# Feed-forward loop one tile longer, clears by range, router weights later, attention's dense products spread over steps

## What is computed

```python
x = x + tanh(g_xattn[0]) * softmax_attention(layernorm(x), ctx)   # 32 heads, 8 groups of keys, head size 16, masks
x = x + tanh(g_ffn[0])   * bit_ffn(layernorm(x))                  # 512 -> 2048 -> 512, ternary weights, gelu
x = x + tanh(g_xattn[1]) * linear_attention(layernorm(x), ctx)    # 16 heads, gated
x = x + tanh(g_ffn[1])   * moe(layernorm(x))                      # shared 2048-wide FFN, and 2 of 8 experts
```

## Time and profile before

| what | value |
|---|---|
| median of 3 runs | 1860.0 us (1858.31 to 1861.89) |
| the profiled execution | 1863.76 us, of it 1862.0 us span |
| granted TensorE clock over the span | 0.954 |
| PE busy | 1620.1 us, 87% |
| DVE, ACT, POOL busy | 964.0, 711.3, 823.7 us |
| phase A, phase B | to 534 us; 541 to 865 us |
| phase C, phase D | to 1120 us; 1124 to 1857.5 us |

### The profile page before, as it was taken

The page is one execution under the profiler, slowest core; times in us unless marked ns, Lnnn a source line. Parts: engine busy times, 40 slices in busy tenths (PEclk is TensorE's granted clock), DMA queues, the critical chain, the costliest instruction groups (busy, mean ns, idle before and its releaser), DMA issues. The chain is left out here.

```text
span 1862.0 us, 29494 instructions
## 1 busy us (share of the span) xinstructions
PE 1620.1 (87%) x10826; PEld 831.9 (45%) x10826; DVE 964.0 (52%) x1947; ACT 711.3 (38%) x1311; POOL 823.7 (44%) x853
## 2 busy tenths in 40 slices
PE   4689998999838888976999987999999999888887
PEld 3255555555413343433665643444444444333343
DVE  5566666667445777761556552376554333111136
ACT  2177778778834444441223221121111111222221
POOL 2377787767733444432344334353343431111134
PEclk9899999999759998998999998999999999999999
DMA  5633444332404444343355425464444652466645
GB/s 180 140 102 92 109 90 104 84 67 65 108 15 91 97 102 99 74 77 62 72 120 102 100 52 139 86 156 108 99 111 97 154 107 61 112 150 157 153 142 170
DMA packets 453941, 195.69 MB, mean 105 GB/s; under 512 B 395484, under 2 KB 418270, under 8 KB 453800
## 3 DMA queue, kind: packets, MB, share of 16 engines
q1 hardware_dynamic: 448120, 175.19, 42.0%
q0 software_dynamic: 5680, 18.62, 3.7%
HBM read 77.17 MB, written 22.81 MB: 54 GB/s over the span
## 5 line engine op out<-in xcount | busy, mean ns | idle before, releaser
L1007 POOL TENSOR_TENSOR a_pl<-a_prob,a_ph 128x512 f16<-128x512 f32 x256 | 295.9, 1169 | 103.8 <-ACT a_prob L916 102.9
L1090 DVE TENSOR_REDUCE a_mx<-bank 128x2 f32<-128x512 f32 x256 | 172.7, 686 | 107.7 <-PE bank L643 105.3
L137 PE MATMUL bank<-XTh,d_whs 128*128 128x512 f16 x512 | 194.8, 380 | 2.1 <-issue 1.3
L138 PE MATMUL bank<-XTl,d_whs 128*128 128x512 f16 x512 | 194.5, 380 | 0.0
L139 PE MATMUL bank<-XTh,d_wls 128*128 128x512 f16 x512 | 194.5, 380 | 0.0
L915 ACT ACTIVATE a_ph<-bank 128x512 f16<-128x512 f32 x256 | 153.7, 601 | 87.5 <-PE bank L663 62.8
L2211 POOL CAST d_cut<-d_raw 128x512 f16<-128x512 f32 x90 | 56.8, 631 | 235.5 <-DMA d_raw<-in_L_ffn_sw 153.9
L916 ACT ACTIVATE a_prob<-bank 128x512 f32<-128x512 f32 x256 | 153.9, 601 | 0.0
L2131 DVE TENSOR_TENSOR d_hid<-d_hid,bank 128x512 f32<-128x512 f32 x64 | 44.0, 687 | 182.9 <-PE bank L139 176.1
L1354 PE MATMUL bank<-b_wpj,b_hTh 128*128 128x512 f16 x256 | 105.5, 412 | 25.6 <-DMA b_hTl<-b_hcut 25.6
L1344 PE MATMUL bank<-b_wfc,b_xTh 128*128 128x512 f16 x256 | 98.3, 384 | 32.6 <-DMA b_xTl<-f_cut 25.5
(11 more groups left out here) (330 smaller groups left out, 3978.7 us busy)
## 6 DMA issues: line engine op xcount, KB each, us to landing
d_raw<-in_L_ffn_w SPq DMA_DIRECT2D x48, 256.0 KB, 3.0
d_raw<-in_L_ffn_sw SPq DMA_DIRECT2D x42, 256.0 KB, 3.1
made<-e_y SPq DMA_DIRECT2D x39, 256.0 KB
a_stage<-in_L_ffn_w_fc SPq DMA_DIRECT2D x32, 256.0 KB, 2.9
a_stage<-in_L_ffn_w_proj SPq DMA_DIRECT2D x32, 256.0 KB, 3.1
a_fbuf<-in_ctx SPq DMA_DIRECT2D x16, 256.0 KB, 3.9
rows<-f_cut SPq DMA_DIRECT2D x16, 256.0 KB, 2.5
out_x<-X SPq DMA_DIRECT2D x16, 256.0 KB
```

The source lines that it names most:

```text
L137: nc.tensor.matmul(out_ap, lhi, rhi, start=first, stop=False)
L138: nc.tensor.matmul(out_ap, lhi, rlo, start=False, stop=False)
L1007: nc.gpsimd.tensor_tensor(pl[:, n % NP, :], prob[:, n % 2, :], ph[:, n % NP, :], ALU.subtract).then_inc(ev["L"], 1)
L1090: nc.vector.tensor_reduce(mx[:, h, tt, half, 2 * (g % 4):2 * (g % 4) + 2], bank[BS + m % 2][:, :].rearrange("p (r k) -> p r k", r=2), AX_X ...
```

## The change

1. `phase` clears each run of neighbouring semaphore numbers with one instruction.
2. Phase A: PQ = (15, 21), PK = (19, 25), OUT = (7, 11), OTURN = (5, 6), TURN0 and NEG0 = 27. Products are cut by k: q and output one k (three matmuls) a step over four steps, kv two k (six short matmuls) a step over two steps. The two halves of the output are turned in two steps. SP's `place_q(b+2, 0)` moves to n = 26.
3. Phase B: `hidden_clip` of a tile moves to the start of the next iteration, `result` into the next iteration, and each engine's order changes; on POOL `low(n+1, 3)` moves behind `dev(m)`.
4. Phase D: the router's transposes and copies move behind step 0.

```diff
-                    for s in held:
-                        pool.sem_clear(s)
+                    for lo, hi in zip(first, after):
+                        pool.sem_clear(range(lo, hi))
...
-    PQ, PK = (10, 14), (12, 16)
-    TURN0, TURN1 = 19, 0
-    NEG0, NEG1 = 18, 4
-    OTURN, OUT = 5, (7, 8)
+    PQ, PK = (15, 21), (19, 25)
+    TURN0, TURN1 = 27, 0
+    NEG0, NEG1 = 27, 4
+    OTURN, OUT = (5, 6), (7, 11)
...
-                    if b + 2 < B and n == TURN0 + 1:
+                    if b + 2 < B and n == PQ[1] + KC + 1:
                         place_q(b + 2, 0)
...
-            def project(dst, xh, xl, w_h, w_l, b, tt, n, what):
+            def project(dst, xh, xl, w_h, w_l, b, tt, n, what, ks):
                 x = slice(tt * P, (tt + 1) * P)
-                for k in range(KC):
+                for k in ks:
                     env["three"](...)
+                if ks[-1] < KC - 1:
+                    return
...
-                    if b and n == OTURN:
+                    for tt in range(2):
+                        if b and n == OTURN[tt]:
...
+                            turn_output(b - 1, tt)
+                        if b and 0 <= n - OUT[tt] < KC:
+                            output(b - 1, tt, [n - OUT[tt]])
...
-                        if n == PQ[tt]:
-                            q_of(b + 2, tt)
-                        if n == PK[tt]:
-                            kv_of(b + 2, tt)
+                        if 0 <= n - PQ[tt] < KC:
+                            q_of(b + 2, tt, [n - PQ[tt]])
+                        if n in (PK[tt], PK[tt] + 1):
+                            kv_of(b + 2, tt, [2 * (n - PK[tt]), 2 * (n - PK[tt]) + 1])
```

ACT's and DVE's parts follow at `PQ[tt] + KC`, `PK[tt] + 2`, `OTURN[tt]` (+1 on DVE) and `OUT[tt] + KC`. Phase B, ACT, POOL and DVE in this order:

```diff
             for n in range(TILES):
                 f = n + LEAD
+                m = n + 2
+                if m < TILES:
+                    gelu(m, 0)
+                    gelu(m, 1)
                 if n + 1 < TILES:
                     high(n + 1)
-                if n + 2 < TILES:
-                    gelu(n + 2, 0)
                 if f < TILES:
                     front_norm(f, 0)
-                if n + 2 < TILES:
-                    gelu(n + 2, 1)
-                    gelu(n + 2, 2)
+                if m < TILES:
+                    gelu(m, 2)
+                    gelu(m, 3)
+                for g in (2 * n, 2 * n + 1):
+                    if g < NG:
+                        high_weight(g)
                 if f < TILES:
                     front_norm(f, 1)
...
+                if m < TILES:
+                    norm(m)
...
-                if n + 1 < TILES:
-                    low(n + 1, 0)
                 if f < TILES:
                     front_dev(f, 0)
                 if n + 1 < TILES:
+                    low(n + 1, 0)
                     low(n + 1, 1)
-                    low(n + 1, 2)
                 if f < TILES:
                     front_dev(f, 1)
                 if n + 1 < TILES:
-                    low(n + 1, 3)
+                    low(n + 1, 2)
                 if n + 2 < TILES:
                     dev(n + 2)
+                if n + 1 < TILES:
+                    low(n + 1, 3)
                 if f < TILES:
                     front_cut(f)
...
-            hidden_clip(1)
             for n in range(TILES):
                 f = n + LEAD
                 m = n + 2
+                if n + 1 < TILES:
+                    hidden_clip(n + 1)
                 if f < TILES:
                     front_moments(f, 0)
...
                     stat(m, 1)
+                if n:
+                    result(n - 1)
                 if f < TILES:
                     front_moments(f, 1)
...
                     stat(m, 3)
                     moments(m)
+                for g in (2 * n, 2 * n + 1):
+                    if g < NG:
+                        low_weight(g)
+                if m < TILES:
                     mean(m)
...
-                result(n)
+            result(TILES - 1)
```

Phase D:

```diff
-            pe.wait_ge(r_in, 32)
-            for k in range(KC):
-                last = nc.tensor.transpose(bank[TR][:, k * E:(k + 1) * E], rw[:, k * P:(k + 1) * P], ident[0:E, 0:E])
-            last.then_inc(r_wt, 1)
+            def turn_router():
...
                 pe_gate(pe, s)
                 pe_up(pe, s)
+                if s == 0:
+                    turn_router()
...
                 dve_low(dve, s)
+                if s == 0:
+                    router()
```

## The result

| | before | after |
|---|---|---|
| median | 1860.6 us (1858.3 to 1861.9) | 1775.5 us (1770.8 to 1778.4) |
| ratio, 95% interval | | 0.954 [0.952, 0.957] |
| profiled execution | 1863.8 us | 1774.6 us, of it 1772.9 us span |
| granted TensorE clock over the span | 0.954 | 0.969 |

The time fell by 85 us, 4.6%. The forecast was 1786 us with a range of 1762 to 1810: direction and range were right, the gain was 11 us larger than its sum of 74.

The account below looks back on a forecast made before the run. PE bounds dense stretches, ACT and POOL light steps, a ring phase B; clears and loads delay phases. Gains of 16.3 (clears), 22 (A), 30 (B) and 5.5 (D) sum to 74 us: from 1860.0 to 1786 us, range 1762 to 1810.

Parts of the forecast that it names:

- Clears, 16.3 forecast: Between phases: 226 single semaphore clears, 16.7 us, become five range clears, 0.4 us; gain 16.3 us.
- Rival (c): Clears: a range clear costs as much as its members, 1802 us; chance 0.05.
- Phase A, 22 forecast: Attention: dense products cut by k let ACT and POOL run beneath PE; iterations 52.2 against 55.8 us, gain 22.
- (b): Phase A: spreading the products gives nothing, ACT and POOL meet their own lumps; A gains 2, 1806 us; chance 0.22.
- (d): Phase A: thinned load lets TensorE's clock fall to 1.2 GHz; three iterations at half clock give 1930 us; chance 0.03.
- The 20 dense steps: Phase A iteration: steps with dense products, 1.6 us each with PE the bound, 32 us, plus bias products about 1.7.
- The two waits: Phase A: PE waits to turn k at step 28, 1.4 us; SP's late transposes and maxima delay step 0, 0.7.
- Phase B, 30 forecast: Feed-forward: period per tile falls from 18.4 to 16.2 us, 12 times, 26.4, plus 4 in the tail; 30 us.
- The ring: Phase B: chain from one norm to the next through clip, statistics and moments, held by POOL's subtractions; 16.2 us.
- The tail: End of phase B: statistics for the next phase come before the last clip; gain 4 us (0 to 6).
- Rival (a): Phase B: DVE's small products win against POOL, B runs at PE's 15.0 us a period; 1772 us, chance 0.20.
- Phase D, 5.5 forecast: Start of phase D: first products no longer wait behind the router's loads, PE starts 5.5 us earlier (3 to 7).

Follow-up runs that it names:

- three tries at step 28: Changed kernel with projections one step earlier, 1777.6 us; with one-input forms and k turned a step later, 1760.6; with forms, earlier projections and earlier maxima, 1764.4.

## Why the prediction was right, point by point

- **Clears, 16.3 forecast, 15.1 by their own rows.** Five ranges, as counted, but I had read from the name that a range costs nothing extra, and it costs more the longer it is. Rival (c) is out.
- **What the pause does to the clock, not in the forecast.** With the shorter pause C starts at full clock, and so does D, for which it takes the router's edit as well. I had read D's start at half clock in the trace and written that it "ran at a granted clock of half either way"; that was wrong, by 0.9 us there (D's first 300 products take 74.2 us instead of 75.1, and 76.3 with the router's edit alone) and by 1.5 to 2 in C.
- **Phase A, 22 forecast, 23 measured.** PE is full from step 7 to 26, the iterations are 52.2, 52.1, 53.1 for the forecast 52.2, and the clock stayed at 1.00, so rivals (b) and (d) are out. The 20 dense steps took 33.75 us for my 33.7. But the working behind the number was right only in part. The two waits were added, 1.4 and 0.7; measured are 1.1 and mostly nothing. The overlap that I gave to all dense steps came from the eight output steps; the projection steps were full either way. And the terms outside b = 1 to 3 cancel: by the means of the executions iteration 0 gained 0.3 us for 1.4, iterations 4 and 5 8 for 6, and 6 and 7 gained 5.4 for 4, and 1 us was lost again outside the iterations. That the sum came out so near is in part luck.
- **Phase B, 30 forecast, 38 measured, the one mis-sized term.** The ring was laid out in the right order, and it is DVE's. From one norm's end I had `dev` done at 12.85, `mean` at 14.05 and the norm at 16.2; the tile above has them at 12.45, 13.6 and 15.7. So 0.4 of the 0.5 us by which the period was too long stand ahead of `dev`, in the sum of clip, statistics and moments, whose instructions follow one another more closely than I added them. The hold itself was right: `mean` ends 1.15 us behind `dev`, with the subtraction. From the second norm to the fourteenth the time fell from 220.7 to 188.3 us, 32.4 for the forecast 26.4: 6 of the 8 us. The tail gave 5.1 behind the last norm (22.7 to 17.6 us until PE starts on the last tile's `down`) for the forecast 4.
- **Rival (a), B at PE's floor.** It didn't happen in the changed kernel, and the holds are why: with them gone B is 13.9 us shorter. The rival was priced at 14, but that was 12 periods from 16.2 to 15.0; measured it was 15.7 to 14.7 and less in the first ones, so the equal number is chance. So is it that 1775.5 lies nearer to the rival's 1772 than to my 1786: by the total alone one would have taken (a) for true, and only the rows of `mean` and the distance of the norms speak against it.
- **Phase D, 5.5 forecast, 6 measured.** 5.2 of it is the earlier first product, the rest the clock.

The rule of the Trainium skill that I had weighed (SBUF — State Buffer, "The single rule") is borne out in both directions: a product of two SBUF tensors is held to the end of POOL's subtraction (1.10 us), one with a single tensor input is not (0.21 us). Its other operand, the per-partition scalar, lies in SBUF as well; by these runs it doesn't count as an input here. By it the ring came out at 15.7, without it B would have run at PE's 14.7.

## What to carry to other kernels

Lay a ring out from the timeline, instruction by instruction, and ask of each small DVE operation which POOL operation runs beside it: a 128x1 product cost 1.10 us in place of 0.15, and a form with a per-partition scalar instead of a second tensor took it away, 14 us of phase B's 286. When two new waits of one loop end come from different queues, don't add them without asking whether they run side by side, and expect the other to appear when one is removed: three tries at step 28 gained nothing. Read a phase's gain from several executions. Cut a dense product over steps where its neighbours are light and PE idles, and look at PE's busy share in each stretch before cutting elsewhere.

## What the runs showed of the hardware that was not expected

- A range clear takes 44 ns for one semaphore and 108, 179, 201, 354 and 547 ns for 13, 28, 32, 60 and 93: 5.0 to 5.5 ns for each further one. Single clears were 74 ns apart.
- TensorE's granted clock after a pause. Phase C began at half clock after 3.78 us of idle PE (six executions) and at full clock after 1.75 to 2.5 (eight); D at half after 5.14 to 9.8 (seven) and at full after 2.3 (seven). But within phase A waits of 1.9 and 2.3 us were followed by 3.4 us at half clock, and others of 2.2 and 2.3 us by none (2.29 us at 193.88 in the run with earlier projections, against 2.34 at 246.55 in the same run), so the length of the pause alone doesn't decide it. This is left open.
- Phases with identical code differ between executions: C by 0.2 us with the long pause ahead of it and by 1.1 with the short one, B by 0.5 to 0.7 and with the one-input forms by 1.7 (270.5 to 272.2), A and D by some 4 us.
